# A graph layer's prologue: three h buffers, tables zeroed early, buckets counted between chunks, form judged last

## What is computed

```python
h = x @ W_in2f
Wij = ssp(f_ij @ W_filt1 + b_filt1) @ W_filt2 + b_filt2      # ssp(v) = softplus(v) - ln 2
Wij = Wij * rcut_ij[:, None]
x_ij = h[idx_j] * Wij                                        # idx_j = dst
agg = segment_sum(x_ij, idx_i, num_segments=n_atoms)         # idx_i = src
out = ssp(agg @ W_out1 + b_out1) @ W_out2 + b_out2
x = layernorm(x + out)
```

## Time and profile before

| | us |
|---|---|
| median of 3 runs | 2367.33 |
| lowest and highest | 2362.75, 2374.13 |
| span of the profiled execution | 2368.4 |
| its edges begin (first L1815) | 109.57 |
| PE, POOL, DVE, ACT busy | 2142.1, 1862.0, 1670.5, 1660.6 |

### The profile page before, as it was taken

One profiled execution on the slowest core, in us unless ns is written; L12 is line 12 of the kernel. 1 busy time (PEld: TensorE's weight loads), 2 busy tenths in 40 slices (PEclk: granted clock), 3 DMA queues, 4 the chain that ended last, 5 costly groups with the idle time before them and its releaser, 6 DMA issues.

```text
span 2368.4 us, 60320 instructions
## 1 busy us (share of the span) xinstructions
PE 2142.1 (90%) x16313; PEld 1410.6 (60%) x16313; DVE 1670.5 (71%) x3879; ACT 1660.6 (70%) x3725; POOL 1862.0 (79%) x1174
## 2 busy tenths in 40 slices
PE   2488999999999999999999999999999999999936
PEld 1365666566666666666666566666666666666613
DVE  5467777768676777767777777777777777777726
ACT  0277777678687777777776777877777777777616
POOL 2078888888888888888888888888888888888874
PEclk8599999999999999999999999999999999999978
DMA  6776665666666666666666666656666566666574
GB/s 208 267 155 95 96 95 90 93 90 100 94 99 92 100 97 95 92 98 97 93 98 93 94 94 94 102 94 96 96 98 91 93 100 95 95 96 91 68 159 130
DMA packets 370945, 250.00 MB, mean 106 GB/s; under 512 B 88788, under 2 KB 350143, under 8 KB 370315
## 3 DMA queue, kind: packets, MB, share of 16 engines
q0 software_dynamic: 160560, 73.14, 32.7%
q1 hardware_dynamic: 199482, 155.27, 27.3%
q10 hardware_dynamic: 10476, 16.77, 1.9%
HBM read 149.90 MB, written 95.13 MB: 103 GB/s over the span
## 4 chain that ended last, share of the span: by engine, by line
DMA 43%; PE 19%; POOL 17%; issue 14%; DVE 3%; ACT 3%; POOLq 0%; SPq 0%; DVEq 0%; ACTq 0%
DMA table<-total,index 40%; POOL table L732 16%; PE unit_psum L1872 5%; PE unit_psum L1891 4%; PE both_psum L1828 3%; PE total_psum L1841 2%; PE pre_psum L1815 2%; DMA h_parts<-h_out 1%; DMA src_g<-in_src 1%; PE both_psum L1853 1%; PE both_psum L1824 1%; ACT out_rows L1122 1%; DVE rank L1249 0%; DVE rank_part L1244 0%; POOL half_sum L776 0%
## 5 line engine op out<-in xcount | busy, mean ns | idle before, releaser
L732 POOL DMA_INDIRECT table<-total,index x1115 | 1803.3, 1617 | 444.8 <-issue 249.0
L1872 PE MATMUL unit_psum<-moving,route_hot 128*128 128x386 bf16 x3136 | 608.8, 331 | 41.0 <-ACT ring L915 36.9
L885 ACT ACTIVATE h_dst<-both_psum,cols 128x128 f32<-128x128 f32 x1564 | 450.2, 386 | 102.4 <-PE both_psum L1853 99.0
L1891 PE MATMUL unit_psum<-scat_hot,ring 64*128 64x448 bf16 x4704 | 481.7, 353 | 9.2 <-DVE scat_hot L1432 6.5
L1872 PEld LDWEIGHTS unit_psum<-moving,route_hot 128*128 128x128 bf16 x3136 | 295.0, 99 | 266.9 <-ACT ring L915 108.2
L915 ACT ACTIVATE ring<-unit_psum 128x386 bf16<-128x386 f32 x784 | 373.5, 509 | 111.8 <-PE unit_psum L1872 70.5
L1828 PEld LDWEIGHTS both_psum<-w_f,hidden 128*128 128x128 f32 x3128 | 415.3, 193 | 18.3
L1828 PE MATMUL both_psum<-w_f,hidden 128*128 128x128 f32 x3128 | 415.7, 276 | 0.0
L1891 PEld LDWEIGHTS unit_psum<-scat_hot,ring 64*128 64x128 bf16 x4704 | 217.0, 95 | 218.5 <-DVE acc_t L1448 7.7
L849 ACT ACTIVATE soft<-pre_psum 128x1024 f32<-128x1024 f32 x196 | 201.9, 1030 | 169.5 <-PE pre_psum L1815 168.6
L1841 PE MATMUL total_psum<-message,same 128*128 128x129 f32 x2232 | 309.5, 281 | 4.8 <-DVE message L1360 4.3
(11 more groups left out here) (116 smaller groups left out, 1599.7 us busy)
## 6 DMA issues: line engine op xcount, KB each, us to landing
dst_b<-dst SPq DMA_DIRECT2D x391, 128.0 KB
src_b<-src SPq DMA_DIRECT2D x279, 128.0 KB
f_t<-in_f_t SPq DMA_DIRECT2D x98, 256.0 KB
table<-total,index POOLq DMA_INDIRECT x1115
table<-zeros ACTq DMA_DIRECT2D x20, 640.0 KB, 5.7
window<-h_parts SPq DMA_DIRECT2D x391, 32.0 KB
parts<-table SPq DMA_DIRECT2D x48, 256.0 KB, 5.2
h_parts<-h_out SPq DMA_DIRECT2D x12, 384.0 KB, 5.4
```

The source lines that it names most:

```text
L732: pool.indirect_dma_start(tables[table], bass.IndirectOffsetOnAxis(index[:, i, k:k + 1], 0), total[:, i, k, 0:DIM], None, compute_op=ALU.a ...
L885: last = act.activation(h_dst[:, b, d], source, ACT.Copy, scale=cols[:, g[1] // HALF % 2, weight:weight + 1])
L1872: last = pe.matmul(unit_psum[:, k % 2, 0:MOVING], route_hot[:, tile, k * P:(k + 1) * P], moving[:, tile, :], start=(tile == 0), stop=(tile ...
L1891: last = pe.matmul(unit_psum[:, strip, 0:BUCKET], ring[rows, r[1] % RING, slot_tile(m), part * DIM:(part + 1) * DIM], scat_hot[rows, r[1] ...
```

## The change

All of it stands before the edges.

- `x_t` gets four buffers and `h_out` three, in space that later holds `x_rows`, behind `zeros`. `h_rest` and `pre_psum` keep two. L810 now waits for the store of the chunk three before. SP loads four chunks of `x_t` at the start and runs four ahead.
- ACT issues the zeroing in three blocks: two copies as before, three after `dst_g` has landed, fifteen after `src_g` has landed, all ahead of chunk 0. `split_h` issues none.
- The bucket counts on PE and the rank steps on DVE are dealt out between chunks 2 to 12 (`BUCKETS_AFTER`: two after chunks 2, 3 and 4, one after each later one). What follows them, `give_slots`, `judge_windows` and `make_biases`, stands after the last chunk.
- The loops over chunks are written out. SP waits for all stores of `h_parts` before it reads the flag, and no more before the first window load.

```diff
+X_BUFFERS, H_BUFFERS = 4, 3
+BUCKETS_AFTER = {2: (0, 1), 3: (2, 3), 4: (4, 5), 5: (6,), 6: (7,), 7: (8,), 8: (9,), 9: (10,), 10: (11,), 11: (12,), 12: (13,)}
...
-        def run_chunks(eng, step, last):
-            step((0, 0), CHUNK // P)
-            step((0, 1), CHUNK // P)
-            with eng.Fori(0, FULL_CHUNKS // 2 - 1) as j:
-                step((j, 2), CHUNK // P)
-                step((j, 3), CHUNK // P)
-            step((0, FULL_CHUNKS), last // P)
+        def run_chunks(step):
+            for i in range(CHUNKS):
+                step((0, i), h_tiles((0, i)))
...
-            load_x_t((0, 0), CHUNK // P)
-            load_x_t((0, 1), CHUNK // P)
+            for i in range(X_BUFFERS):
+                load_x_t((0, i), CHUNK // P)
...
-            with sp.Fori(0, FULL_CHUNKS // 2 - 1) as j:
-                for b in range(2):
-                    load_x_t((j, b + 2), CHUNK // P)
-                    store_h((j, b), CHUNK // P)
-            load_x_t((0, FULL_CHUNKS), LAST_H // P)
-            store_h((0, FULL_CHUNKS - 2), CHUNK // P)
-            store_h((0, FULL_CHUNKS - 1), CHUNK // P)
-            store_h((0, FULL_CHUNKS), LAST_H // P)
+            for i in range(CHUNKS):
+                if i + X_BUFFERS < CHUNKS:
+                    load_x_t((0, i + X_BUFFERS), h_tiles((0, i + X_BUFFERS)))
+                store_h((0, i), h_tiles((0, i)))
+            for b in range(H_BUFFERS):
+                sp.wait_ge(h_stored[b], last_stored(b))
             sp.wait_ge(flag_made, 1)
...
+            act.wait_ge(dst_loaded, 16)
+            for fifth in range(2, FIFTHS):
+                zero(0, fifth)
+            act.wait_ge(src_loaded, 16)
+            for k in range(1, TABLES):
+                for fifth in range(FIFTHS):
+                    zero(k, fifth)
+
             def split_h(c, tiles):
-                b = c[1] % 2
-                if not isinstance(c[0], int):
-                    for k in range(1 + b, TABLES, 2):
-                        zero(k, c[0])
-                else:
-                    zero(0, min(2 + c[1], FIFTHS - 1))
+                b, q = c[1] % 2, c[1] % H_BUFFERS
                 act.wait_ge(h_mm, after_chunk(c))
-                previous(act, h_stored[b], c, landed_chunk)
+                if c[1] >= H_BUFFERS:
+                    act.wait_ge(h_stored[q], landed_chunk(plus(c, -H_BUFFERS), H_BUFFERS))
...
                 if is_at(c, 1):
                     place_routed()
-                    judge_windows()
-                    make_biases()
-
-            run_chunks(dve, split_h, LAST_H)
+                for bucket_number in BUCKETS_AFTER.get(c[1], ()):
+                    rank_in_bucket(bucket_number)
+
+            run_chunks(split_h)
+            give_slots()
+            judge_windows()
+            make_biases()
...
                 last.then_inc(h_mm, 1)
-                if is_at(c, 1):
-                    count_in_buckets()
-
-            run_chunks(pe, node_features, LAST_H)
+                count_in_buckets(BUCKETS_AFTER.get(c[1], ()))
+
+            run_chunks(node_features)
+            pe.wait_ge(meta_step, META_STEPS + 4)
+            pe.matmul(unit_psum[0:1, 0, 0:1], crowded[:, 0:1], ones_col[:, 0:1], start=True, stop=True
+                      ).then_inc(crowd_mm, 1)
             pe.wait_ge(bias_made, 6)
```

More of the change, by code:

```diff
@@ L274, in summed, with landed_chunk, h_tiles, last_stored @@
     return ADDS * after_chunk(c)
-def landed_chunk(c):
-    return 16 * c[0] + 16 * (c[1] // 2 + 1)
+def landed_chunk(c, n=2):
+    return 16 * c[0] + 16 * (c[1] // n + 1)
+def h_tiles(c):
+    return LAST_H // P if c[1] == CHUNKS - 1 else CHUNK // P
+def last_stored(b):
+    return landed_chunk((0, max(i for i in range(CHUNKS) if i % H_BUFFERS == b)), H_BUFFERS)
 def is_chunk(c):
@@ L438, in build @@
         bias_mm, bias_made = sem("bias_mm"), sem("bias_made")
-        x_t_loaded = [sem(f"x_t_loaded{b}") for b in range(2)]
+        x_t_loaded = [sem(f"x_t_loaded{b}") for b in range(X_BUFFERS)]
         h_mm, h_hi, h_left, h_mid, h_lo = (sem(n) for n in ("h_mm", "h_hi", "h_left", "h_mid", "h_lo"))
-        h_stored = [sem(f"h_stored{b}") for b in range(2)]
+        h_stored = [sem(f"h_stored{b}") for b in range(H_BUFFERS)]
         f_loaded = [sem(f"f_loaded{b}") for b in range(2)]
@@ L761, in _ @@
                 pool.wait_ge(cols_made, 2)
-                for b in range(2):
-                    pool.wait_ge(h_stored[b], 16 * (FULL_CHUNKS // 2 + (b == 0)))
+                for b in range(H_BUFFERS):
+                    pool.wait_ge(h_stored[b], last_stored(b))
                 run_groups(pool, step_general)
@@ L1239, in place_routed, with rank_in_bucket, give_slots @@
                 assert steps == META_HOTS
[L1240 to L1251, removed]
+            def rank_in_bucket(b):
+                steps = META_HOTS + (0 if b == 0 else 2 * b - 1)
+                dve.wait_ge(meta_mm, b + 1)
+                part = rank if b == 0 else rank_part
+                dve.wait_ge(meta_step, steps)
+                dve.tensor_tensor(part[:, :], unit_psum[:, b % 2, 0:ROUTES * TILES], in_bucket[:, b, :], ALU.mult
+                                  ).then_inc(meta_step, 1)
+                if b:
+                    dve.wait_ge(meta_step, steps + 1)
+                    dve.tensor_tensor(rank[:, :], rank[:, :], rank_part[:, :], ALU.add).then_inc(meta_step, 1)
+            def give_slots():
+                steps = META_STEPS - 2
                 dve.wait_ge(meta_step, steps)
@@ L1768, in _, with count_in_buckets @@
                       ).then_inc(bias_mm, 1)
-            def count_in_buckets():
-                for b in range(BUCKETS):
+            def count_in_buckets(numbers):
+                for b in numbers:
                     counts = unit_psum[:, b % 2, 0:ROUTES * TILES].rearrange("p (g k) -> p g k", k=TILES)
@@ L1782, in count_in_buckets @@
                     last.then_inc(meta_mm, 1)
-                pe.wait_ge(meta_step, META_STEPS + 4)
-                pe.matmul(unit_psum[0:1, 0, 0:1], crowded[:, 0:1], ones_col[:, 0:1], start=True, stop=True
-                          ).then_inc(crowd_mm, 1)
             def node_features(c, tiles):
-                b = c[1] % 2
-                pe.wait_ge(x_t_loaded[b], landed_chunk(c))
+                b, q = c[1] % 2, c[1] % X_BUFFERS
+                pe.wait_ge(x_t_loaded[q], landed_chunk(c, X_BUFFERS))
                 previous(pe, h_left, c, after_chunk)
-                x3 = x_t[:, b, 0:tiles * P].rearrange("d (p k) -> d k p", k=tiles)
+                x3 = x_t[:, q, 0:tiles * P].rearrange("d (p k) -> d k p", k=tiles)
                 for k in range(tiles):
```

22 lines of the change are left out of this document (10 added, 12 removed).

## The result

The changed kernel takes **2404.9 us** (median of 4 runs, 2401.75 to 2410.13), the kernel before 2365.0 beside it: a ratio of 1.0162, with an interval of 1.0144 to 1.0181. It is 1.6% slower. The forecast was 2376.7, from 2357 to 2384, so the time lies outside the range. The profiled execution took 2402.0 us, 33.6 more than that of before.

A forecast was written before the change was run, and what follows sets the result against it. The edges rule the span; DVE's and the DMA engines' stages, one behind the other, set their start. Chunk 3 at 73.1 + 44.2 + 1.66 = 119.0, 9.4 us later than before: median 2376.7 us, range 2357 to 2384.

The forecast's parts named there:

- What costs nothing: Side effects: with chunk loops unrolled, no engine waits on code in the first 110 us; bounds 0 and 2 us.
- The start of the edges: First L1815 matmul on PE: at 119.0 us against 109.57, 9.4 us later.
- src_g: Load of src_g, ahead of all chunks: lands at 32.1 us, not 27.1.
- The two x_t loads: Two more x_t loads on SP ahead of src_g, 512 KB: 1.3 us of delay to it.
- the early zeros: Zero packets taking turns with weight_c and src_g on six DMA engines: 18 more, 3.6 us.
- Chunk 3: Chunk 3's L1287 on DVE, waiting for chunk 0's store behind the zeros: starts at 73.1 us after 18 us idle.
- From there to DVE's end: DVE's remaining chunks, 12 buckets and closing steps after chunk 3's L1287: 44.2 us, ending at 117.3.
- Behind DVE's end: Gap from DVE's end to PE's first matmul of the edges: kept at 1.66 us.
- A: Forecast case: chunk 0's store is late, zeros passing packet for packet on six engines; 2370 to 2382 us, chance 0.56.
- C: Rival: ACT itself is held by its outstanding copies; 10 to 24 us slower, middle 2383.3 us; chance 0.10.
- D: Rival: the long edges take up or absorb a 10 us shift of their start; 2363 to 2371 us, chance 0.10.
- B: Rival: SP queue not held, DVE the bound; edges start at 101.0, median 2358.7 us, 2355 to 2364; chance 0.24.

The follow-up runs named there:

- e1: The changed kernel with 125 extra waiting instructions on PE ahead of its first chunk; 2372.4 us, ratio 1.0027.
- e2: The kernel before with 131 extra waiting instructions on PE ahead of the bucket counts, none of the change; 2398.8 us, ratio 1.0134.
- e10: The changed kernel with only the head of PE's loop over units placed at slot 16 of 256; 2374.2 us, ratio 1.0033.
- e4: The changed kernel with the zeroing dealt out over the chunks again and 125 extra PE instructions; 2355.8 us, ratio 0.9954.
- e9: As e4, but with the head of PE's loop placed at slot 16 instead of the 125 extra instructions; 2358.0 us, ratio 0.9956.
- e5: The kernel before with all zeroing issued early as in the changed kernel, and nothing else; 2374.3 us, ratio 1.0044.
- e7: As e4, with x_t of chunks 2 and 3 loaded behind src_g and the index broadcasts behind chunk 2's store; 2361.1 us, ratio 0.9982.
- e12: As e9, with x_t of chunks 2 and 3 loaded behind src_g and the index broadcasts behind chunk 2's store; 2353.1 us, ratio 0.9941.
- e8: The changed kernel with 125 extra PE instructions and the index broadcasts behind the store of chunk 2; 2370.5 us, ratio 1.0026.
- e11: As e9, with a hint for the closing branch as the first instruction of each pass of PE's loop; 2357.7 us, ratio 0.9948.
- e6: As e4, but with all 14 buckets counted and ranked behind chunk 1; 2368.1 us, ratio 1.0014.
- e3: The changed kernel with 32 extra waiting instructions on PE ahead of its first chunk; 2374.5 us, ratio 1.0037.

## Why the prediction was wrong

**The failed step stands under "What costs nothing": "The loops unrolled: no engine waits on code in these 110 us; bounds 0 and 2 us."** In these 110 us nothing measured speaks against it, and it was the wrong place to look. Code placed ahead of a loop moves the loop, and the loop is 2200 us long. The row that could have warned me was in the trace of before: 32.5 us of "issue" at L1824, thirteen times, 2.5 each. I hadn't asked what that was. Its priced size would still have needed a run, but the bound above wasn't 2 us: the same wait once more in each pass is 13 x 2.5 = 32. e1, e2 and e10 show the cause from both sides: some 30 us of the 39.9 between the medians (38 by the ratio), where the sum had nothing.

**The start of the edges, forecast 119.0, was 113.69.** Its terms, from the changed kernel's DVE and PE:

```profile
31.11 1.23 DVE L1173 CAST src_g<-src_g 102x2048 uint16<-102x2048 int32 x1 [11.65 <-DMA src_g<-in_src]
...
70.85 0.69 DVE L1297 TENSOR_TENSOR h_rest<-pre_psum,h_out 128x512 f32<-128x512 f32 x1 [1.39 <-ACT h_out L816]
...
83.19 0.68 DVE L1297 TENSOR_TENSOR h_rest<-pre_psum,h_out 128x512 f32<-128x512 f32 x1
...
86.38 0.69 DVE L1297 TENSOR_TENSOR h_rest<-pre_psum,h_out 128x512 f32<-128x512 f32 x1
...
111.73 0.91 DVE L1216 COPY bias_o<-bias_hi 1x512 bf16<-1x512 bf16 x3
```

- src_g: 32.1 forecast, 31.1 measured, and that is luck, for both terms were off. The two x_t loads were given 1.3 us and the early zeros 3.6. With the x_t loads ahead of it and the zeros in turns, src_g is cast at 30.65 (e4) and 31.03 (e9); with the zeros early and no x_t ahead, at 26.58 (e5); with neither, at 27.08 (before), 26.7 (e7) and 27.1 (e12). The x_t loads cost 4 us, the early zeros next to nothing. e5 and e4:

```profile
26.58 1.23 DVE L1170 CAST src_g<-src_g 102x2048 uint16<-102x2048 int32 x1 [7.98 <-DMA src_g<-in_src]
```

```profile
30.65 1.23 DVE L1171 CAST src_g<-src_g 102x2048 uint16<-102x2048 int32 x1 [11.81 <-DMA src_g<-in_src]
```

- Chunk 3: 73.1 forecast, 70.85 measured.
- From there to DVE's end: 44.2 forecast, 41.8 measured. A chunk with one bucket takes 3.19 (83.19 to 86.38), not 2.04 + 1.39: beside a chunk a bucket costs 1.15.
- Behind DVE's end: 1.66 forecast, 1.05 measured (112.64 to 113.69).

The three differences, 2.2, 2.4 and 0.6, are the 5.3 us.

**A, the late store, held, but it was one of two.** Packets do pass one for one where both queues have work for the same engines, and nearly all zeros were written before chunk 0's store. The two hardware queues of the changed kernel at 25 to 29, 62 to 68 and 68 to 72:

```profile
q1 hardware_dynamic: 50, 0.41, 24.1%
q10 hardware_dynamic: 50, 0.23, 13.6%
...
q1 hardware_dynamic: 708, 1.26, 59.5%
q10 hardware_dynamic: 173, 0.76, 30.6%
...
q1 hardware_dynamic: 414, 0.95, 63.0%
q10 hardware_dynamic: 21, 0.08, 4.7%
```

The last zeros (q10) fade out at 68 to 72, and the store is seen at 70.22, where I had 72.4. The Trainium skill, DMA: Bandwidth & Descriptors, section on queues, rings and completion order, gives a coarser turn, of 9 to 17 descriptors; 50 packets over the six engines of src_g are eight each, and with such turns they would hardly come out equal, so that 50 to 50 and 116 to 116 speak for single packets. The order of the packets' starts says it outright: from 20 to 22.6 us of the kernel before they alternate one by one, 4 bytes on q10, 8192 bytes on q1.

**C, ACT held by its own issues, happened.** I gave 0.42 us for an issue, 6.3 for fifteen. ACT and SP in the changed kernel:

```profile
13.57 39.32 ACTq L791 DMA_DIRECT2D table<-zeros  x18
52.94 0.60 ACT L816 ACTIVATE h_out<-pre_psum 128x512 bf16<-128x512 f32 x1 [44.22 <-issue]
...
70.22 0.60 ACT L816 ACTIVATE h_out<-pre_psum 128x512 bf16<-128x512 f32 x1 [3.41 <-DMA h_parts<-h_out]
```

```profile
36.92 3.68 SPq L571 DMA_DIRECT2D f_t<-in_f_t  x2
...
46.58 0.33 SPq L576 DMA_DIRECT2D dst_b<-dst  x1
46.95 1.19 SPq L582 DMA_DIRECT2D src_b<-src  x1
48.18 1.26 SPq L576 DMA_DIRECT2D dst_b<-dst  x1
...
55.86 1.05 SPq L541 DMA_DIRECT2D h_parts<-h_out  x1
```

Fifteen copies between 31.1 and 52.9 are 1.45 us each, three and a half times my price, and SP's small broadcasts took 1.2 to 1.3 at the same time, where the first took 0.33 before. The first L816 was at 52.94, not 38.4. It stayed below the 56.4 up to which I had said that A hides it, and e8 shows how close the two are: with the store out of the way the start moves by 0.6 us. The 11.52 us of the earlier trace rows had been a warning, and I had set it aside because its packets were more. SP's first dst_b was at 46.58 (forecast 50 to 54), and DVE had not 15 to 18 us idle ahead of chunk 3 but 1.39: it had waited before, at chunk 0, for ACT (21.2 us).

**D, that the edges take a shift up, is refuted.** Kernels without the second stall, in the order of their start:

| | start, us | against 109.57, us | ratio | ratio less 1, in us of 2366 |
|---|---|---|---|---|
| e12 | 94.09 | -15.5 | 0.9941 | -14.0 |
| e4 | 96.68 | -12.9 | 0.9954 | -10.9 |
| e9 | 98.09 | -11.5 | 0.9956 | -10.4 |
| e11 | 98.55 | -11.0 | 0.9948 | -12.3 |
| e7 | 103.65 | -5.9 | 0.9982 | -4.3 |
| e6 | 111.97 | +2.4 | 1.0014 | +3.3 |
| e8 | 113.08 | +3.5 | 1.0026 | +6.2 |
| e1 | 113.71 | +4.1 | 1.0027 | +6.4 |
| e3 | 113.84 | +4.3 | 1.0037 | +8.8 |
| e10 | 113.99 | +4.4 | 1.0033 | +7.8 |
| e5 | 120.37 | +10.8 | 1.0044 | +10.4 |

A microsecond of the start is about a microsecond of the time, within 4.5 us; the intervals are 3 to 5 us either way. Nine of the eleven lie 1 to 4.5 us above what their start gives, which stays unexplained. So the change without the stall would have been within the forecast (2374.2 in e10, where 2376.7 was given), and that partly by luck: its start was 4.4 us later and not 9.4, and the time 7.8 us longer.

**B, the gain, was there to be had.** Filling DVE's gaps with rank steps was forecast to start the edges at 101.0 if nothing held the chunks. With the zeroing in turns they start at 96.7 and 98.1. The change gave it away by zeroing early (17 us, e4): it held ACT at its issues until 52.94, and it made SP wait longer for the store of src (issued at 32.36, first dst_b at 46.58; in e4 at 31.91 and 38.70), and so for chunk 0's.

What stays open: that the second stall is a fetch of code is a reading of the packets of q8 (12 or 13 more) and of the place of the head, which e1, e2, e3 and e10 show to matter; no run shows whether the 4.0 us are one fetch that starts only when the branch is taken, or two that wait for one another. The runs tell where the head must not lie relative to before, not at which slot of a block that is, nor why a fetch takes this long.

## What to carry to other kernels

Before you call an edit ahead of a long loop free, look for "issue" waits at that loop's head, and count the instructions that the edit adds on the engine: on an engine near its limit, 131 instructions in a prologue cost 30 us in a loop that nobody had touched, and placing the loop's head gave them back. When a change is slower by more than the part that it touches, compare equal stretches outside of it first. A bulk transfer that isn't urgent should be dealt out behind the urgent ones: issued all at once, it holds the issuing engine and, packet for packet, what the other queue has on the same engines. And when a forecast of a part comes out right, look whether its terms did: src_g came when it was forecast, with both terms wrong.

## What the runs showed of the hardware

- Where a loop's head lies decides whether PE stalls a second time in each pass: 4.0 us, some five matmuls behind the head. Counted from the kernel before, a loop shifted by 0, some 163 (e3) or some 256 instructions (e1) doesn't stall there, nor one whose head is placed (e10); one shifted by some 131 does, with the change (the changed kernel) and without (e2). The Trainium skill, in the section named above, calls the crossing of a block "mostly hidden"; if the second stall is such a crossing, right behind a taken branch it isn't, by these 4.0 us. It also holds that kernels "prefer full unrolling where possible"; here the unrolling of another loop brought the stall.
- The stall at the head (2.5 us a pass) goes away with a hint for the branch (e11), and with it 12 packets of q8 (149 in e11, 161 in e9).
- An instruction on PE that only waits for what has long come takes 0.1 us: 12.3 for 125.
- Issuing a plain copy from ACT took 0.42 us (two in 0.85) and 1.45 in a row of fifteen of 640 KB; SP's took 1.2 to 1.3 at the same time.
- Two queues with work for the same DMA engines pass packet for packet: 50 to 50 and 116 to 116, and one by one in order of start from 20 to 22.6 us of the kernel before.
- A load ahead of another can cost more than its bytes: two x_t loads of 256 KB put src_g 4 us later (30.65 in e4, 26.71 in e7), where by the prediction's 25 GB/s for each engine they are 1.3.
